# Scatters of the last pair issued in four portions ahead of additions 40 to 43, in a Mamba-2 and mixture-of-experts kernel on one core

## The reference

```
h = layernorm(x) * (1 + ca) + sa
x = x + ga * mamba2(h)            # state-space scan, 4 heads of 64, state 128
h = layernorm(x) * (1 + cb) + sb
x = x + gb * moe(h)               # 8 experts, the 2 best of each token, weights softmax of the 2
```

## Time and profile before

| what | value |
|---|---|
| median of 3 runs | 825.5 us (823.67 to 825.77) |
| the profiled execution | 832.36 us, span from first to last instruction 830.5 us |
| busy: PE, DVE, ACT, POOL | 82%, 67%, 62%, 56% of the span |
| mean granted clock of TensorE | 0.916 of full speed |

### The profile page before, as it was taken

One profiled execution on the slowest core, in us unless ns is written; L12 is line 12 of the kernel. 1 busy time (PEld: TensorE's weight loads), 2 busy tenths in 40 slices (PEclk: granted clock), 3 DMA queues, 4 the chain that ended last, 5 costly groups with the idle time before them and its releaser, 6 DMA issues. The chain is left out here.

```text
span 830.5 us, 13734 instructions
## 1 busy us (share of the span) xinstructions
PE 680.6 (82%) x3713; PEld 518.9 (62%) x3713; DVE 559.4 (67%) x1640; ACT 516.8 (62%) x1223; POOL 462.0 (56%) x366
## 2 busy tenths in 40 slices
PE   3678899789789999998999999999966952774982
PEld 3246557556567776876787777768755731553662
DVE  2827967988986997898689978987743561231421
ACT  3784795896796899687969977886522310221320
POOL 2003004444453378757775786688687477357775
PEclk9779798999998999999999999999996967897997
DMA  5100001112013465455346444653645774857973
GB/s 186 28 0 1 1 27 32 45 52 71 33 58 102 119 168 129 105 155 125 92 105 174 107 97 103 204 104 90 180 107 120 200 204 95 202 123 149 191 169 28
DMA packets 81275, 88.86 MB, mean 107 GB/s; under 512 B 7360, under 2 KB 67696, under 8 KB 81200
## 3 DMA queue, kind: packets, MB, share of 16 engines
q1 hardware_dynamic: 54528, 61.37, 25.6%
q0 software_dynamic: 26672, 26.62, 18.0%
HBM read 54.50 MB, written 33.46 MB: 106 GB/s over the span
## 5 line engine op out<-in xcount | busy, mean ns | idle before, releaser
L457 POOL DMA_INDIRECT out<-xs x142 | 226.8, 1597 | 116.9 <-issue 53.2
L427 POOL DMA_INDIRECT rows<-payload,pos x128 | 131.6, 1028 | 68.2 <-issue 30.2
L880 DVE SCALAR_TENSOR_TENSOR xbc<-T,table,xbc 128x511 f32<-128x511 f32 (+2 forms) x192 | 141.9, 746 | 7.7 <-ACT xbc L599 3.1
L1133 DVE SCALAR_TENSOR_TENSOR xs<-FX,xs 128x128 f32<-128x128 f32 x142 | 43.1, 345 | 122.6 <-PE FX L1457 104.7
L1457 PE MATMUL FX<-wt,hid 128*128 128x128 f32 x568 | 87.8, 301 | 17.2 <-DVE hid L1125 17.2
L655 ACT ACTIVATE xt<-FX 128x256 f32<-128x256 f32 x71 | 27.0, 380 | 110.1 <-PE FX L1434 96.0
L1457 PEld LDWEIGHTS FX<-wt,hid 128*128 128x128 f32 x568 | 73.7, 203 | 26.6 <-DVE hid L1125 17.9
L648 ACT ACTIVATE sg<-FG,wt 128x256 f32<-128x256 f32 x142 | 59.3, 471 | 47.0 <-PE FG L1444 38.4
L1444 PE MATMUL FG<-xt,wt 128*128 128x256 f32 x284 | 77.6, 397 | 12.1 <-DMA wt<-in_wt 8.1
L1287 PE MATMUL T<-h,win 128*128 128x512 f32 x128 | 76.7, 698 | 12.4 <-DVE xbc L880 10.6
L1444 PE MATMUL FV<-xt,wt 128*128 128x256 f32 x284 | 78.2, 400 | 0.0
(11 more groups left out here) (207 smaller groups left out, 1343.5 us busy)
## 6 DMA issues: line engine op xcount, KB each, us to landing
wt<-in_wt SPq DMA_DIRECT2D x71, 386.0 KB
xs<-rows SPq DMA_DIRECT2D x71, 258.0 KB
x<-in_x SPq DMA_DIRECT2D x8, 512.0 KB, 4.3
out<-x SPq DMA_DIRECT2D x8, 512.0 KB
out<-xs POOLq DMA_INDIRECT x142
rows<-pad SPq DMA_DIRECT2D x8, 258.0 KB
rows<-payload,pos POOLq DMA_INDIRECT x128
gate_a<-gates SPq DMA_DIRECT2D x8, 128.0 KB, 4.3
```

The source lines that it names most:

```text
L427: pool.indirect_dma_start(d["rows"], bass.IndirectOffsetOnAxis(ap=pos[:, k, n:n + 1], axis=0), payload[:, n, :], None).then_inc(scattered, 16)
L457: pool.indirect_dma_start(d["out"], bass.IndirectOffsetOnAxis(ap=xs[:, t % XSR, c, PAY - 1:PAY].bitcast(U32), axis=0), xs[:, t % XSR, c, 0 ...
L880: last = nc.vector.scalar_tensor_tensor(out=xbc[:, t, k, tap:L], in0=T[:, k, 0:L - tap], scalar=w, in1=xbc[:, t, k, tap:L], op0=ALU.mult, ...
```

## The change

Three places change. On POOL the scatters of pair 7 leave the common pattern: `last_scatters` issues two calls (four DMAs) ahead of each of the additions 40, 41, 42 and 43, with `second_weight` ahead of the third portion; additions 44 and 45 follow directly. On DVE `new_tiles(7)` stands behind `expert_out(42)`; it stood behind `expert_out(44)`. On PE `expert_turn(49)` stands behind `expert_down(48)`; it stood ahead of it.

```diff
+            def last_scatters(p):
+                t = PT * (p + 1) - 24
+                for n in range(4):
+                    if n == 2:
+                        second_weight(p)
+                    scatter(p, 2 * n)
+                    scatter(p, 2 * n + 1)
+                    add_out(t + n)
+                add_out(t + 4)
+                add_out(t + 5)
+
             for i in range(-2, 13):
-                if is_pair(i - 2):
+                if 0 <= i - 2 < NP - 1:
                     scatter(i - 2, 7)
...
                 if is_tile(PT * i - 25):
                     add_out(PT * i - 25)
+                if i == NP:
+                    last_scatters(i - 1)
+                    continue
...
                 if is_tile(PT * i - 22):
                     expert_out(PT * i - 22)
+                if i == NP:
+                    new_tiles(i - 1)
...
-                if is_pair(i - 1):
+                if 0 <= i - 1 < NP - 1:
                     new_tiles(i - 1)
...
-                if is_tile(PT * i - 15):
+                if is_tile(PT * i - 15) and PT * i - 15 != NTILES - LAST:
                     expert_turn(PT * i - 15)
                 if is_pair(i):
                     turn_h2(i)
                 if is_tile(PT * i - 16):
                     expert_down(PT * i - 16)
+                if PT * i - 15 == NTILES - LAST:
+                    expert_turn(PT * i - 15)
```

## The result

The changed kernel takes 831.84 us (median of 4 runs, 831.59 to 833.57) against 824.59 us before (4 runs): ratio 1.0092, 95% interval 1.007 to 1.0115. It is 7.2 us slower. The forecast was 827.1 us, 1.6 us slower, with a difference too small to tell as the likeliest outcome (46%). The time lies inside the stated range (822.5 to 832) by 0.2 us, but the slowdown is more than four times the one forecast.

The account below looks back on a forecast made before the run. The prediction took POOL's chain of additions, each waiting for the last to land, as the bound. Unfilled gaps put addition 47 2.1 us later, less 0.5 behind it: 825.5 + 1.6 = 827.1 us, range 822.5 to 832.

Parts of the forecast that it names:

- What bounds the kernel: In the tail, POOL's additions each wait for the one before to land; PE, despite standing still 19.18 us, is not awaited.
- rival C: At the end of the kernel: PE sets the end, so the tail is 12.5 us shorter, 813 us; chance 6%.
- B: Rival on POOL: all gaps short at 2.65 us, also those behind additions 47 and 48; -5.5 us, 820 us; chance 17%.
- POOL up to addition 43: On POOL: first scatter 0.96 us after the positions, landings covered by scatters, addition 43 starting at 687.4, last scatter 17.3 us earlier.
- The turn of tile 49: On PE: rows 49 asked for after the padding lands, about 694.4; turn at 697.1, 12.5 us earlier; swap costs nothing.
- The four gaps: On POOL behind additions 43 to 46: unfilled waits of 4.4, 3.3, 2.8 and 3.26 us, together 13.8; addition 47 2.1 us later.
- Behind addition 47: On POOL: gap of 4.2 us instead of 4.70 because weights 50 go before, gaining 0.5 us; 5.03 behind addition 48 stays.
- Sum: Whole kernel: +2.1 at addition 47 less 0.5 behind it gives +1.6 us, 827.1 us on the median.
- its sign of being wrong: On POOL: addition 47 starting over 2.5 us from 714.9, or an addition of tiles 44 to 56 waiting for DVE's result.
- The case: Whole kernel: the forecast's mechanism at 55%, own range -1 to +4.5 us, 824.5 to 830, against the rivals.
- Rival A: On POOL: the load does not thin out, four gaps total 19.8 us instead of 13.8; +7.6 us, 833 us; chance 22%.

## Why the prediction was wrong, step by step

- **What bounds the kernel.** Right. PE turned tile 49 ten microseconds earlier and nothing at the end moved with it; rival C is out, and so is B: the gaps ahead of additions 48 and 49 stayed at 4.8 to 5.5 and 4.4 to 4.6.
- **POOL up to addition 43.** Right: first scatter +0.97 (forecast +0.96), additions 40 to 43 at +6.1, +15.0, +24.7, +33.6 (forecast +6.1, +15.1, +24.8, +33.8).
- **The turn of tile 49.** Forecast +43.5, measured +45.8. The padding was issued at +28.7, forecast +27.3.
- **The four gaps.** This is the step that failed, in size: 13.8 us were taken, 15.3, 15.4, 12.1 and 16.0 measured in four traces, mean 14.7. The last two terms (2.8 and 3.26) fit (2.4 to 3.1, and 3.0). The first two, the ones in the padding's traffic, were 4.4 and 3.3 and came out at 5.7 to 6.0 and 3.8 to 4.8 in three traces of four. The text said that the early list "buys nothing" and gave it no price of its own beyond the 4.4; on top of the portions it costs 3.4 ± 1.8 us. With the list at its old place the four gaps were 12.1 to 12.4. For the changed kernel the text's own row, 5.73 us behind addition 43 with the padding in flight, was the better guess.
- **Behind addition 47.** 4.2 was taken for the gap behind it; 5.48, 4.86, 4.80 and 5.22 were measured. The 0.5 us credited for weights gone earlier were not there.
- **Sum.** Addition 47 was forecast at +61.3 and came at +62.7, +62.8, +59.8 and +63.7, mean 62.2, each within the 2.5 us that the text had set as its sign of being wrong. The sign did not trip although the total was missed, because it was tied to a single trace of before. Addition 47 stands at 59.2 there and at 58.0 on the mean of three; so the difference of the means at addition 47 is 4.2 us where 2.1 was forecast, 0.9 of the miss from the gaps and 1.2 from that base. At addition 51 the means are 92.1 and 87.8, a difference of 4.3 (forecast 1.6), since the credited 0.5 us was not there; at the end of the span they are 180.2 and 175.1, a difference of 5.1. The ratios of the three timed comparisons (0.77 to 0.93% of 825) say 6.4 to 7.7. The remaining 1 to 3 us are within the scatter of executions and are not located.
- **The case.** Rival A had the direction, the same mechanism and nearly the time (833), but priced the four gaps at 19.8. In three traces of four the truth lay between it and the forecast, past the 14.7 at which the text itself had put the border to a slowdown that can be told; in the fourth it was 12.1. 22% for A, against 55% for a case that straddled the border by its own range, was too little. That the range holds the measured time is owed to the part of it that was put there for A; the forecast's own ended at 830.

## What to carry to other kernels

In this kernel an accumulating DMA that must have landed before the next one may start leaves POOL a gap (2.4 to 6.0 us), and independent DMA issues of that engine are free only inside such gaps: gathering them ahead of one point takes them from the gaps behind it, which cost 0.3 to 0.5%. Before moving work earlier because an engine is seen idle, ask whether the end of the program waits for that engine; here a 19 us hole on PE was slack. And a stretch whose length hangs on how transfers meet should be profiled more than once before its single gaps are used as prices: the same gap, with two scatters ahead of it, was 0.9, 3.1 and 3.5 us in three executions of one kernel.

## What was not expected of the hardware

Two DMAs of 128 rows, added to HBM, took 2.4 to 6.0 us from the end of their descriptors to the start of the next addition. Where SP had last asked for the rows of one or two tiles (ahead of addition 46, portions of two calls) it was 2.4 to 3.1; where it had just asked for the rows of one tile and the weights of two (ahead of addition 48), 4.6 to 5.5. But the changed kernel showed 3.49 in one execution and 5.65 to 6.01 in three at the same place, ahead of addition 44, and the cause of the two values is open. In every kernel that issues the scatters in four portions of two calls the time from the start of addition 70 to the end of the span is 8.2 to 8.4 us (829.6 - 821.30 in the rows above), in all others 7.8 to 8.0. Nothing tried explains these 0.4 us.
